# A four-layer graph network on one core: edges bucketed by TensorE instead of by scattered DMA, bfloat16 counts and gcn products

## The reference

```python
edge_index = jnp.stack([src, dst])
h = jnp.maximum(_layernorm(x, axis=-1), 0.0)
x = x + _L0_gnn_ref(h, src, dst, edge_weight, L0_gnn_w_self, L0_gnn_w_neigh)
h = jnp.maximum(_layernorm(x, axis=-1), 0.0)
x = x + _L1_gnn_ref(h, L1_gnn_W1, L1_gnn_b1, L1_gnn_W2, L1_gnn_b2, edge_index)
h = jnp.maximum(_layernorm(x, axis=-1), 0.0)
x = x + _L2_gnn_ref(h, edge_index, edge_weight, L2_gnn_W, L2_gnn_b)
h = jnp.maximum(_layernorm(x, axis=-1), 0.0)
x = x + _L3_gnn_ref(h, L3_gnn_W0, L3_gnn_b0, L3_gnn_W1, L3_gnn_b1, edge_index, edge_type_8)
```

## Time and profile before

| what | us |
|---|---|
| median of 3 runs (2971.26 to 2975.32) | 2972.81 |
| the profiled execution (its span) | 2974.7 |
| PE busy in it | 2562.7 |
| DVE, ACT, POOL busy | 1254.7, 537.0, 1291.0 |
| loading and ranking, to the first one-hots | 0 to 138 |
| sage with building | 138 to 795 |
| gcn1 / gcn2 | 804 to 947 / 951 to 1122 |
| hop1 and hop2 | 1122 to 1870 |
| relation layers | 1870 to 2975 |

### The profile page before, as it was taken

How to read it: one execution, slowest core, us unless ns; L and a number is a source line. 1 busy time by engine, 2 the same in 40 slices (tenths; PEclk the granted TensorE clock), 3 DMA queues, 4 the chain that set the end, 5 groups by cost and what they waited for, 6 DMA issues and landing times.

```text
span 2974.7 us, 37615 instructions
## 1 busy us (share of the span) xinstructions
PE 2562.7 (86%) x11805; PEld 2031.2 (68%) x11806; DVE 1254.7 (42%) x2688; ACT 537.0 (18%) x1584; POOL 1291.0 (43%) x1271
## 2 busy tenths in 40 slices
PE   4699999999799999999999999588888876666666
PEld 3488888888799998888777776355555544444444
DVE  4888888888321442111233333233333422222222
ACT  0255555555200000000111112111111110000000
POOL 2787777770000000000000000577777747777776
PEclk9899999999899999999999999799989987787787
DMA  2033333333398774444444443444545443333333
GB/s 92 4 136 136 132 125 133 137 137 135 136 297 297 244 244 153 150 150 154 132 137 139 141 145 104 150 147 146 160 146 160 146 129 110 109 111 109 111 109 94
DMA packets 168353, 426.05 MB, mean 143 GB/s; under 512 B 39048, under 2 KB 102646, under 8 KB 168082
## 3 DMA queue, kind: packets, MB, share of 16 engines
q1 hardware_dynamic: 57052, 258.59, 25.2%
q0 software_dynamic: 53248, 109.98, 13.4%
q10 hardware_dynamic: 57910, 55.64, 5.4%
HBM read 284.37 MB, written 139.73 MB: 143 GB/s over the span
## 4 chain that ended last, share of the span: by engine, by line
PE 60%; POOL 25%; issue 9%; DVE 3%; DMA 1%; ACT 1%; SPq 1%; PEldq 0%; DVEq 0%; POOLq 0%; PEld 0%; ACTq 0%
PE agg L880 28%; POOL gathered L635 25%; PE y L767 9%; PE agg L788 9%; PE y L726 7%; PE prod L719 3%; PE agg L927 1%; PE turn_ps L704 1%; SPq L459 1%; DMA gathered<-in_edge_weight 1%; PE y L685 1%; DMA gathered<-table_rel,idx_rel 0%; PE y L681 0%; PE y L719 0%; DVE stream L1215 0%
## 5 line engine op out<-in xcount | busy, mean ns | idle before, releaser
L635 POOL DMA_INDIRECT gathered<-table_rel,idx_rel x832 | 797.1, 958 | 1493.1 <-DMA table_rel<-gathered 1240.2
L927 PE MATMUL agg<-gathered,onehot 128*128 x2048 | 594.7, 453 | 283.5 <-SPq L554 212.9
L927 PEld LDWEIGHTS agg<-gathered,onehot 128*128 128x128 f32 x2048 | 454.1, 227 | 427.8 <-issue 353.2
L880 PE MATMUL agg<-t_sb,stream 128*128 128x128 f32 (+1 forms) x3750 | 563.2, 312 | 14.7 <-issue 7.8
L598 POOL DMA_INDIRECT edges_bucketed<-edges,pos_u x416 | 488.6, 1174 | 175.9 <-issue 124.1
L880 PEld LDWEIGHTS agg<-t_sb,stream 128*128 128x128 f32 x3750 | 526.3, 193 | 48.6 <-issue 15.2
L1577 DVE SCALAR_TENSOR_TENSOR onehot<-iota,tilebase,edges 128x256 f32<-128x256 f32 x512 | 243.4, 485 | 721.2 <-PE agg L927 697.3
L767 PE MATMUL y<-gathered,relw 128*128 128x256 f32 x1300 | 336.0, 382 | 14.6 <-ACT gathered L1032 12.1
L788 PE MATMUL agg<-h_sb,stream 128*128 128x257 f32 x1250 | 320.4, 381 | 0.0
L767 PEld LDWEIGHTS y<-gathered,relw 128*128 128x128 f32 x1300 | 246.5, 191 | 49.8 <-ACT gathered L1032 15.2
L973 ACT COPY turned<-turn_ps 128x256 f32<-128x256 f32 (+2 forms) x100 | 39.8, 398 | 1301.6 <-PE turn_ps L704 1300.0
(11 more groups left out here) (157 smaller groups left out, 1497.2 us busy)
## 6 DMA issues: line engine op xcount, KB each, us to landing
table_rel<-y_sb ACTq DMA_DIRECT2D x176, 256.0 KB, 3.3
stream<-counts_dense SPq DMA_DIRECT2D x50, 832.0 KB, 4.6
stream<-weights_dense SPq DMA_DIRECT2D x50, 832.0 KB, 4.4
stream<-counts_dense SPq DMA_DIRECT2D x50, 768.0 KB, 4.4
stream<-weights_dense SPq DMA_DIRECT2D x50, 768.0 KB, 4.4
weights_dense<-stream SPq DMA_DIRECT2D x25, 832.0 KB, 3.4
counts_dense<-t_sb SPq DMA_DIRECT2D x25, 832.0 KB, 5.1
weights_dense<-stream SPq DMA_DIRECT2D x25, 768.0 KB, 5.1
```

The source lines that it names most:

```text
L635: pool.indirect_dma_start(gathered[:, slot * D:(slot + 1) * D], None, tables[n], bass.IndirectOffsetOnAxis(ap=idx_rel[:, c:c + 1], axis=0) ...
L880: mm = pe.matmul(sums(n, t)[:, 0:width], stream[:, at % 2, s * P:(s + 1) * P], table(n, s), start=s == 0, stop=s == TILES - 1)
L927: mm = pe.matmul(agg[b][:, 0:width], onehot[:, half_ * QUAD + k, :], gathered[:, bass.ds((q & (GQ - 1)) * (QUAD * D) + k * D, width)], sta ...
```

## The change

The scattered DMAs and the bucketed array go. `slots_of(t)` on DVE makes, for the 25 chunks in which tile t's edges can lie, one-hots of an edge's slot (3,200 elements) and of its bucket (650); `value_buckets(t)` on GpSimd multiplies the latter by five bfloat16 fields of the edge (source, destination and the weight in three pieces; 3,250 elements); `permute(t)` on PE multiplies the two, 25 products of 130 columns into PSUM; `take_tile(t)` on DVE copies the result to `recs` and adds the weight's pieces. `localize` and the DVE sum of one-hots go. A build is now a float32 product of 128 columns for the weight and a bfloat16 one of 128 columns for the count, which reads the upper halves of the float32 one-hots with a step of two; degrees are one bfloat16 product of one column per bucket. Of three banks ACT copies two and DVE one. Counts are stored as bfloat16. The gcn tables are split into three bfloat16 pieces (gcn1's by GpSimd in `split`, gcn2's by DVE), so a product is 384 columns of bfloat16, with one more per tile for the node itself; DVE adds the pieces up (`add_pieces`). Counts are loaded a tile at a time into four buffers. Edge arrays are loaded as 96 + 7 + 1 rows, src and dst from SP's queue and weight and type from ACT's. The tables of hop1 and hop2 swap buffers, and the last three tiles of relation rows instead of four have buffers of their own.

The diff, cut to its core:

```diff
-        return at % 2, at // 2 + 1
+        return (1, at // 3 + 1) if at % 3 == 2 else (0, at // 3 * 2 + at % 3 + 1)
...
+    def window(t):
+        return max(0, E * t // N - MARGIN), min(CHUNKS, -(-E * (t + 1) // N) + MARGIN)
...
-            load_edges(src, flat_i[:, 0:F], s_src)
-            load_edges(dst, flat_i[:, F:2 * F], s_dst)
-            load_edges(edge_type, flat_i[:, 2 * F:3 * F], s_edge)
-            load_edges(edge_weight, flat_w, s_edge)
+            load_edges(sp, src, flat_i[:, 0:F], s_src)
+            load_edges(sp, dst, flat_i[:, F:2 * F], s_dst)
...
+            def value_buckets(t):
+                lo, hi = window(t)
+                wide = hi - lo
+                pool.wait_ge(slots_ready, t + 1)
+                nc.gpsimd.tensor_tensor(valued[:, 0:wide, :, :],
+                                        bucket_hot[:, 0:wide, :].unsqueeze(2).broadcast_to([P, wide, FIELDS, BCK]),
+                                        fields[:, lo:hi, :].unsqueeze(3).broadcast_to([P, wide, FIELDS, BCK]), ALU.mult
+                                        ).then_inc(values_ready, 1)
...
+            def split(n, to, t, k):
+
+                pool.wait_ge(whole_ready, k + 1)
+                made(nc.gpsimd.tensor_copy(pieces[to][:, t, 0, :], whole))
+                made(nc.gpsimd.tensor_tensor(remains, whole, pieces[to][:, t, 0, :], ALU.subtract))
+                made(nc.gpsimd.tensor_copy(pieces[to][:, t, 1, :], remains))
+                made(nc.gpsimd.tensor_tensor(remains, remains, pieces[to][:, t, 1, :], ALU.subtract))
+                made(nc.gpsimd.tensor_copy(pieces[to][:, t, 2, :], remains))
+                pool.sem_inc(S[n, "table_ready"], 1)
...
+            for t in range(TILES + 6):
+                if t < TILES:
+                    value_buckets(t)
+                if t >= 6:
+                    split("sage", "gcn1", t - 6, t - 6)
...
-                    buckets = [s - lo] + [hi - lo] * (s == t)
-                    for j, bucket in enumerate(buckets):
-                        mm = pe.matmul(bank[:, k * D:(k + 1) * D], src_hot[:, h % 2, bucket, :],
-                                       pair_hot[:, h % 2, bucket, :, :].rearrange("p k d -> p (k d)"),
-                                       start=j == 0, stop=j == len(buckets) - 1)
+                    for at_ in [s - lo] + [hi - lo] * (s == t):
+                        pe.matmul(bank[:, k * D:k * D + P], src_hot[:, h % 2, at_, :], pair_hot[:, h % 2, at_, 0, :],
+                                  start=first, stop=True, skip_group_check=True)
+                        first = False
+                        mm = pe.matmul(bank[:, k * D + P:(k + 1) * D], upper(src_hot[:, h % 2, at_, :]),
+                                       upper(pair_hot[:, h % 2, at_, 1, :]), start=False, stop=True,
+                                       skip_group_check=True)
                 mm.then_inc(built, 1)
...
-            def degrees(t):
-
-                pe.wait_ge(sum_made, 2 * t + 2)
-                for k in range(2):
-                    pe.matmul(sums("sage", t)[:, D + 1:D + 2], hot_sum[:, (2 * t + k) % 4, :], ones[:, 0:1],
-                              start=False, stop=True, skip_group_check=True)
+            def degrees(h):
+
+                t, part = h // 2, h % 2
+                lo, hi = PARTS[part]
+                if part == 0:
+                    pe.wait_ge(sum_free, t + 1)
+                    pe.wait_ge(perm_read, min(t + 2, TILES))
+                buckets = hi - lo + (lo <= t < hi)
+                for at_ in range(buckets):
+                    mm = pe.matmul(sums("sage", t)[:, DEG:DEG + 1], upper(pair_hot[:, part, at_, 1, :]), ones_b[:, 0:1],
+                                   start=part == 0 and at_ == 0, stop=True, skip_group_check=True)
+                mm.then_inc(deg_done, 1)
+
+            def permute(t):
+                lo, hi = window(t)
+                pe.wait_ge(slots_ready, t + 1)
+                pe.wait_ge(values_ready, t + 1)
+                if t >= 3:
+                    pe.wait_ge(sum_free, t)
+                for c in range(hi - lo):
+                    mm = pe.matmul(perm_ps[t % 2], slot_hot[:, c, :], valued[:, c, :, :].rearrange("p f s -> p (f s)"),
+                                   start=c == 0, stop=c == hi - lo - 1, skip_group_check=True)
+                mm.then_inc(permuted, 1)
...
+                if i < HALVES:
+                    degrees(i)
                 if i % 2:
-                    if i < HALVES:
-                        degrees(i // 2)
+                    if (i + 3) // 2 < TILES:
+                        permute((i + 3) // 2)
...
+                        if part == 1 and n in ("gcn1", "gcn2"):
+                            mm = pe.matmul(sums(n, t)[:, 0:width], ident_b[:], table(n, t), start=False, stop=True,
+                                           skip_group_check=True)
...
+            load_edges(act, edge_weight, flat_w, s_edge)
+            load_edges(act, edge_type, flat_i[:, 2 * F:3 * F], s_edge)
...
+            def slots_of(t):
+                lo, hi = window(t)
+                wide = hi - lo
+                prep(nc.vector.scalar_tensor_tensor(own_slot[:, 0:wide], tile_b[:, lo:hi], float(t), slot1[:, lo:hi],
+                                                    ALU.is_equal, ALU.mult))
+                if t >= 1:
+                    dve.wait_ge(permuted, t)
+                nc.vector.tensor_tensor(bucket_hot[:, 0:wide, :],
+                                        bucket[:, lo:hi].unsqueeze(2).broadcast_to([P, wide, BCK]),
+                                        iota[:, 0:BCK].unsqueeze(1).broadcast_to([P, wide, BCK]), ALU.is_equal)
+                nc.vector.tensor_tensor(slot_hot[:, 0:wide, :],
+                                        iota1[:].unsqueeze(1).broadcast_to([P, wide, P]),
+                                        own_slot[:, 0:wide].unsqueeze(2).broadcast_to([P, wide, P]), ALU.is_equal
+                                        ).then_inc(slots_ready, 1)
+
+            def take_tile(t):
+
+                rec = recs[:, t % RECS, :, :]
+                if t >= RECS:
+                    dve.wait_ge(dw_ready, 2 * (t - RECS) + 2)
+                dve.wait_ge(permuted, t + 1)
+                prep(nc.vector.tensor_copy(rec.rearrange("p f s -> p (f s)"), perm_ps[t % 2]))
+                dve.sem_inc(perm_read, 1)
+                prep(nc.vector.tensor_tensor(rec[:, 2, :], rec[:, 2, :], rec[:, 3, :], ALU.add))
+                prep(nc.vector.tensor_tensor(rec[:, 2, :], rec[:, 2, :], rec[:, 4, :], ALU.add))
...
-                if what == "sum":
-                    dve.wait_ge(cnt_ready, h + 1)
-                    nc.vector.tensor_reduce(hot_sum[:, h % 4, :],
-                                            pair_hot[:, h % 2, 0:count + own, 1, :].rearrange("p b d -> p d b"),
-                                            AXX, ALU.add).then_inc(sum_made, 1)
...
+                if i % 2 == 0:
+                    if (i + 2) // 2 < TILES:
+                        take_tile((i + 2) // 2)
+                    if (i + 4) // 2 < TILES:
+                        slots_of((i + 4) // 2)
...
+            def add_pieces(n, t, freed):
+                of = sums(n, t)
+                step(nc.vector.tensor_copy(post[:, 0:HID], of[:, 0:HID]))
+                step(nc.vector.tensor_tensor(post[:, 0:HID], of[:, HID:2 * HID], post[:, 0:HID], ALU.add))
+                step(nc.vector.tensor_tensor(post[:, 0:HID], of[:, 2 * HID:3 * HID], post[:, 0:HID], ALU.add))
+                dve.sem_inc(freed, 1)
...
-                step(nc.vector.tensor_scalar(table("gcn2", t), post[:, 0:HID], 0.0, d(t, 0), ALU.max, ALU.mult))
+                step(nc.vector.tensor_scalar(post[:, 0:HID], post[:, 0:HID], 0.0, d(t, 0), ALU.max, ALU.mult))
+                to = pieces["gcn2"][:, t, :, :]
+                step(nc.vector.tensor_copy(to[:, 0, :], post[:, 0:HID]))
+                step(nc.vector.tensor_tensor(post[:, 0:HID], post[:, 0:HID], to[:, 0, :], ALU.subtract))
+                step(nc.vector.tensor_copy(to[:, 1, :], post[:, 0:HID]))
+                step(nc.vector.tensor_tensor(post[:, 0:HID], post[:, 0:HID], to[:, 1, :], ALU.subtract))
+                step(nc.vector.tensor_copy(to[:, 2, :], post[:, 0:HID]))
```

326 lines of the change are left out of this document (174 added, 152 removed).

## The result

The changed kernel took 3185.48 us (median, 3180.43 to 3187.35), against 2974.07 us for the kernel of before in the same series (2971.26 to 2975.79): a ratio of 1.0706, 95% interval 1.0691 to 1.0721, slower by 7%. The profiled execution has a span of 3178.6 us, 203.9 more than before. The forecast was 3082 in a range of 2990 to 3200: the sign and the range held, and the value was 103 us short.

A forecast was written before the change was run, and what follows sets the result against it. PE was taken to bound the sage stage, gcn1 and gcn2. Sage +173 + 10 - 2, start -11, gcn1 -36.5, stop -7 and gcn2 -17 on 2974.7 made 3084, or 3082 us on the median's scale; range 2990 to 3200.

The forecast's parts named there:

- PE's own work: Sage stage: PE's work a tile, with changed builds, degrees and permutation, would be 24.9 us instead of 25.3.
- The head of the even round: Sage stage, DVE: take_tile and slots_of ahead of the update add 5.35 us uncovered; PE stands 6.2 us an even round.
- Clock: Sage stage, behind PE's stand: some 5.5 us of work at half speed, 2.8 us lost, of which 2.3 count.
- rival C: Sage stage: GpSimd's product and DVE's two-input steps hold each other, +36 to +128 us, middle 3164; chance 0.25.
- A: The main forecast, with the head uncovered and the clock falling in the sage stage: 3082 us, chance 0.38.
- Rival B: Sage stage: the same stall with the clock kept, 31.65 us a tile, +6.35; 3036 us, chance 0.15.
- Rival D: Sage stage: DVE's new work finds cover and PE's 24.9 us a tile sets the pace; 2892 us, chance 0.18.
- ACT's larger share: Sage stage evictions: ACT copies two banks of three, 2.2 more evictions of 0.65 us a tile, at no cost.
- Start: Before the first one-hots: edge loads -26 us, new work +15 (between 11 and 20), together -11.
- gcn1, gcn2: bfloat16 products: -36.5 us in gcn1, -7 at the stop before gcn2, -17 in gcn2, where DVE holds the tile.

The follow-up runs named there:

- e9: The kernel of before, no edit, run again in the third series: 2974.81 us, sage stage ending at 792.4 us.
- e8: Changed kernel reordered: ACT copies every bank, DVE none, slots_of last, GpSimd's product later; sage ends at 764.8 us, 3246.46 us, ratio 0.8545 to before.
- e6: Changed kernel with DVE making the slot one-hots twice in each slots_of: sage ends at 1147.9 us, ratio 0.9566 to before in its series.
- e1: Changed kernel with GpSimd's product waiting for DVE's destination one-hots of the even round: sage ends at 950.3 us, 32.93 us a tile.
- e7: Changed kernel with 180 unused bfloat16 products on PE before the fourth group of even rounds of tiles 4 to 23: sage ends at 1040.1 us.
- e2: Changed kernel with GpSimd's product written as five instructions of five chunks instead of one: sage ends at 990.7 us, 34.62 us a tile.
- e10: The kernel of before with only the changed kernel's edge loads: 2948.33 us, ratio 0.9917 to before.
- e12: As e8, but GpSimd's product starts as soon as slots_of is through: 2904.86 us, sage ends at 785.3 us, ratio 0.9769 to before.
- e4: Changed kernel with take_tile behind the source one-hots, slots_of behind the evictions, GpSimd's product after the odd round's destination one-hots: sage ends at 846.4 us.
- e5: The changed kernel again, no edit, in the second series: 3550.49 us, sage ends at 1064.4 us, ratio 0.9343 to before.

## Why the prediction was right, and where it was short

**What bounds the kernel, and PE's own work.** Held. The kernel of before stays at 2974 (e9), and PE's own tile, forecast at 24.9, is 24.47 where PE is full (e8). By terms: a build 0.33 instead of 0.32; 13 degree products 0.47, so 0.9 a tile instead of 1.3; the permutation 1.62 instead of 1.5. The sum had a slip of 0.2: its own terms (25.3 - 2.9 + 1.3 - 0.5 + 1.5) make 24.7.

**The head of the even round.** Held, and shown: 3.4 us a tile for 3.48 us more of it (e6), and with the head and no hold the stage is 164 us longer than before (e1, from its first one-hots at 131.1 to 950.3: 819.2 against 655.2). The forecast for it was 181. The odd round was forecast at 11.85 us and takes 11.9 (719.5 to 731.4).

**Clock.** The mechanism held, the size did not: the term took 2.3 us a round, and e7 gives 1.5. How long the clock stays down was forecast well: in the 19 rounds it was at 0.50 for 3.1 to 6.4 us of PE's work behind the stand, 4.7 on average, for a forecast of 5.5 from the ranking. The round from 710.4 us, shown above, is the shortest of them. In the next even round, where PE resumed at 748.1, the clock is back only 6.4 us later, in the second of these stretches:

```profile
752.00:754.00 2.00, 2.00 (x7) 1.66 (x8) 0.76 (x2) 2.00 (x8) 0.00 (x0) 0.50 0.00 0
754.00:756.00 2.00, 2.00 (x13) 1.78 (x12) 0.00 (x0) 0.91 (x3) 0.00 (x0) 0.88 0.00 0
```

Of the 2.3 us of work that this loses, 1.5 count, as ACT's weighing is near behind (e7); the working had let 2.3 of 2.8 count for that reason.

**The term that was short: the hold.** The sum took DVE's update as done 10.4 us behind the permutation and left GpSimd's product to rival C, with a chance of 0.25. It was done at 15.8 (693.7 to 709.5), inside the 12.2 to 16.8 that C gave. e1 prices it at 113 us (C: 36 to 128, middle 82), e2 shows it to go by the instruction. So the stage is A's with 1.5 for the clock (181 - 20 x 0.8 = 165; e1 has 164), and C on top: 278 of the 279 us. C's two ends had put 1.5 and 2.3 us of the update behind the product; it is 3.2 (706.33 to 709.5), because the step held is already the tile's own one-hot or the first scaling. That 3200 was the top of the range was partly luck: A's terms don't reach 3185, and the range held because it took in most of C. The row that C rested on, a DMA issue of GpSimd that took 2.56 us beside a DVE comparison instead of 0.96, was the only kind of sign in the trace of before, but not a single row: of 347 such issues from 150 to 670 us, 86 began inside a one-hot comparison of DVE's and 83 of these took over 1.1 us, up to 2.64; of the other 261, also those beside DVE's sums and copies, none took over 0.97. It showed GpSimd waiting for DVE, and the working left open whether DVE waits for GpSimd. It does: whoever begins second waits. The Trainium skill (SBUF — State Buffer, Who interferes with whom) says so, and this case's rows agree, down to which steps are held: two-input one-hots (7.22 us for 1.89), a float32 `tensor_scalar` over 256 or 2 elements (5.83 for 0.35, 5.04 for 0.17) and a two-input step of 2 elements (0.88 for 0.16), but neither a `tensor_scalar` of one element nor copies out of PSUM. The scaling of two elements in the changed kernel:

```profile
550.53 5.04 DVE L1368 TENSOR_SCALAR small<-small 128x2 f32<-128x2 f32 x1
```

For the product's own time the Trainium skill (GPSIMD Engine Reference, Elementwise — side-by-side cycle accounting) gave an estimate of 7.0 us. The trace doesn't bear it out: alone the product took 5.64 us (e1), and the 7.08 of the changed kernel hold a wait for DVE's first step. Had I weighed C by the rule, or by all its rows, C would have been the likeliest, at 3164.

**Rival B** (clock kept) fell with the changed kernel's trace, where the clock is at 0.50 behind each of the 19 stands, and with e7. **Rival D** (the head costs nothing) fell with e6; its time, 2892, is that of the change's parts once the order gives them cover: e8's estimate is 2883.5 of span, 2885 on the scale of the medians.

**ACT's larger share** cost nothing, as said, and more than that: e8 gives ACT all the banks, and PE is full.

**Start.** -8.4 for a forecast of -11. The last edge array is used at 10.45 us instead of 37.61, 27.2 earlier (forecast 26); the new work ahead of the first one-hots took 18.7 of them back (forecast 15, with 11 to 20 as bounds). e10 has the loads without that work: 25.5 us.

**gcn1, gcn2.** -43.1 and -19.0 for -43.5 and -17. The gcn2 tile, forecast at 6.05 and held by DVE, in a row each of PE's turn, of the product before it and of the next (two of its tiles on PE, timeline):

```profile
1204.42 0.33 PE L960 MATMUL agg<-gathered,ident_b 128*128 128x384 bf16 x1
1205.25 0.33 PE L754 MATMUL turn_ps<-ident,post 128*128 128x128 f32 x1 [0.51 <-DVEq L1616]
...
1210.53 0.33 PE L960 MATMUL agg<-gathered,ident_b 128*128 128x384 bf16 x1
1211.37 0.33 PE L754 MATMUL turn_ps<-ident,post 128*128 128x128 f32 x1 [0.51 <-DVEq L1616]
```

It is 6.11 us, and what PE waits for is DVE, as the forecast had it.

## What to carry to other kernels

A new step is priced by the place it takes in its engine's queue, not by the engine's total: DVE's own work stayed what it was (1250.5 us busy in e1, 1254.7 before), and yet e1's sage stage is 25% longer (819.2 for 655.2 us), because 5.3 us of new steps (693.83 to 699.08 in the changed kernel) stand ahead of the one update that releases the banks. In the changed kernel it is 43% longer, as 5.4 us of standing through GpSimd's product (7.39 for 2.03) come behind them. When work is given to GpSimd, list what DVE does beside it, and put the long GpSimd instruction where DVE's next two-input step is waited for by nobody, or cut it in pieces. The same parts, in an order found by asking for each step who waits for it, gave a kernel 7% slower than before, 2.3% faster (e12) or, by the estimate above, 3% faster (e8).

## What the runs showed of the hardware that I had not expected

On the chips of the first two series the kernel of before took 3839.69 and 3834.15 us instead of 2974, the changed one 3550.49 instead of 3185. In the changed kernel's family all of it lies in the relation layers, with their 832 gathers by indirect DMA. That stage in the first trace of the changed kernel, and in e4 (columns as above):

```profile
2085.00:3178.00 1093.00, 780.24 (x2498) 532.08 (x2498) 326.31 (x662) 69.84 (x125) 796.97 (x832) 0.85 0.44 129
```

```profile
1868.00:3340.00 1472.00, 786.82 (x2498) 535.30 (x2498) 326.13 (x662) 69.83 (x125) 794.55 (x832) 0.74 0.32 96
```

The engines do the same work in 379 us more: GpSimd issues as fast, but waits, in e4 for 327 us (1.8 in the first trace) until PE has used rows, with PE's granted clock at 0.74 instead of 0.85. What makes PE use them later isn't shown. The kernel of before lost 495 us on top of that, and it is the one with 416 more indirect DMAs, the scatter of the edges, which the change takes out; no trace of it was taken on such a chip, so that these make the difference is argued, not shown. What is shown is that the sign of this change differs between two series on two chips: 1.0706 on the first, 0.9343 on the chip of e5. Whether it is the chip or something else that differed at the time was not tested. A change that swaps DMAs for work on the engines should be timed on more than one chip.
